# A bias added to the residual rows in the expert groups instead of in the attention windows, and one written order per engine

## The reference

```
x = x + tanh(g_xattn) * gamma * attention(layernorm(x), ctx, ctx)   # 8 heads of 16, softmax over 512
u = layernorm(x)
h = u @ down_w + down_b                                             # 512 -> 256
gate, top 2 of 8 experts = softmax(u @ router_w + router_b - cost)
moe = sum over the two of gate_k * (gelu(gelu(h) @ w1_e + b1_e) @ w2_e + b2_e)  # unchosen experts add a constant
moe = moe + 0.1 * (gelu(gelu(h) @ shared_w1 + b) @ shared_w2 + b)
out = x + tanh(g_ffn) * (moe @ up_w + up_b + gelu(u) @ core_w + core_b)
```

## Time and profile before

| what | value |
|---|---|
| median of 3 runs | 758.85 us (758.62 to 760.65) |
| the profiled execution's own time | 758.85 us |
| its span, first to last instruction | 757.0 us |
| mean granted TensorE clock | 0.992 |
| busy: PE | 699.4 us, 92% |
| busy: DVE | 520.9 us, 69% |
| busy: ACT | 539.5 us, 71% |
| busy: POOL | 487.4 us, 64% |

### The profile page before, as it was taken

One profiled execution on the slowest core, in us unless ns is written; L12 is line 12 of the kernel. 1 busy time (PEld: TensorE's weight loads), 2 busy tenths in 40 slices (PEclk: granted clock), 3 DMA queues, 4 the chain that ended last, 5 costly groups with the idle time before them and its releaser, 6 DMA issues.

```text
span 757.0 us, 20840 instructions
## 1 busy us (share of the span) xinstructions
PE 699.4 (92%) x6134; PEld 379.1 (50%) x6134; DVE 520.9 (69%) x834; ACT 539.5 (71%) x1117; POOL 487.4 (64%) x480
## 2 busy tenths in 40 slices
PE   0699999999999999999898999999999999999978
PEld 0122222333233232223364555588888888888634
DVE  1999998999999999998776456544444444444345
ACT  1389988999999989998765565577667676676311
POOL 5648688888888888868476141346666666566521
PEclk9999999999999999999999999999999999999989
DMA  6545556655565555553437742788889988776666
GB/s 200 201 135 183 187 173 193 206 184 172 196 198 193 190 184 189 177 166 128 127 130 256 263 139 104 248 145 123 123 116 123 124 125 108 101 108 81 144 177 235
DMA packets 137953, 124.04 MB, mean 164 GB/s; under 512 B 70164, under 2 KB 108820, under 8 KB 137880
## 3 DMA queue, kind: packets, MB, share of 16 engines
q1 hardware_dynamic: 123672, 107.50, 49.3%
q0 software_dynamic: 13632, 15.47, 14.2%
q10 hardware_dynamic: 576, 0.13, 0.1%
HBM read 60.39 MB, written 51.53 MB: 148 GB/s over the span
## 4 chain that ended last, share of the span: by engine, by line
PE 61%; DVE 9%; DMA 9%; issue 8%; POOL 6%; ACT 4%; SPq 2%; DVEq 0%; POOLq 0%; ACTq 0%
PE EH L1190 23%; PE Y L1190 15%; PE pv L531 8%; PE ring L518 6%; DVE mx L653 4%; PE nat L506 4%; DMA QS<-q_scratch 3%; ACT P L592 2%; DMA y_sums<-ysb,to 2%; POOL ao L707 1%; SPq L387 1%; DVE statx L635 1%; PE ring L550 1%; DMA q_scratch<-qhl 1%; POOL un L704 1%
## 5 line engine op out<-in xcount | busy, mean ns | idle before, releaser
L653 DVE TENSOR_REDUCE mx<-nat 128x2 f32<-128x1024 f32 x256 | 298.3, 1214 | 31.4 <-PE nat L506 30.4
L592 ACT ACTIVATE P<-ring 128x512 f32<-128x512 f32 x512 | 276.7, 605 | 18.9 <-PE ring L518 11.2
L1956 POOL DMA_INDIRECT y_sums<-ysb,to x84 | 138.2, 1645 | 98.1 <-DVE ysb L1894 85.3
L531 PE MATMUL pv<-P,VT 128*32 128x256 f32 x2048 | 158.5, 393 | 0.3
L506 PE MATMUL nat<-KS,QS 48*128 48x512 f16 x512 | 110.3, 396 | 29.9 <-DMA KS<-k_scratch 16.0
L518 PE MATMUL ring<-QS,KS 49*128 49x512 f16 x512 | 120.9, 391 | 10.3 <-ACT P L592 9.1
L1521 ACT ACTIVATE X<-EH,bcur 128x256 f32<-128x256 f32 x168 | 85.7, 560 | 52.8 <-DVE u L1857 49.0
L1190 PE MATMUL EH<-XA,whi 128*128 128x256 f16 x672 | 116.9, 273 | 0.5 <-DMA XA<-g_rows 0.5
L1190 PE MATMUL Y<-whi,u 128*128 x672 | 116.9, 273 | 0.3 <-DVE u L1857 0.3
L1857 DVE TENSOR_TENSOR u<-X,u 128x512 f16<-128x512 f32 x84 | 57.8, 688 | 78.9 <-ACT u L1527 78.9
L1190 PE MATMUL EH<-XA,wlo 128*128 128x256 f16 x336 | 91.6, 273 | 0.0
(11 more groups left out here) (259 smaller groups left out, 1013.4 us busy)
## 6 DMA issues: line engine op xcount, KB each, us to landing
XA<-in_wall SPq DMA_DIRECT2D x8, 800.0 KB, 4.5
u<-in_wall SPq DMA_DIRECT2D x8, 800.0 KB, 4.4
QS<-q_scratch SPq DMA_DIRECT2D x64, 96.0 KB, 2.3
KS<-k_scratch SPq DMA_DIRECT2D x64, 96.0 KB, 2.4
X<-in_x SPq DMA_DIRECT2D x16, 256.0 KB, 2.7
X<-in_ctx_kv SPq DMA_DIRECT2D x16, 256.0 KB, 3.2
q_scratch<-qhl SPq DMA_DIRECT2D x16, 256.0 KB, 2.1
k_scratch<-khl SPq DMA_DIRECT2D x16, 256.0 KB, 2.2
```

The lines of the kernel that those rows point to most:

```text
L531: m = pe.matmul(pv[32 * j:32 * j + 32, q], VT[i][:, lb, g, j, :], Pb[4 * (s % 2) + j][:, q], start=(lb == 0 and half == 0), stop=(lb == 3) ...
L592: act.activation(Pb[4 * (s % 2) + j][:, :], bank[:, :], ACT.Exp).then_inc(t_use.sem, 1)
L653: dve.tensor_reduce(mx[:, k // 8, :, k % 8], nat[k % 2][:, :, :], AX.X, ALU.max).then_inc(t_max.sem, 1)
L1956: pool.indirect_dma_start(out=ysum[:, :], out_offset=bass.IndirectOffsetOnAxis(ap=to[:, j % 2, a:a + 1], axis=0), in_=ysb[j % 2][:, a, :], ...
```

## The change

- x1t is gone from GpSimd's list. The rows x1 are stored without tb, as soon as x1 is there: the store stands before the load of xr in SP's window, a window's part earlier than the layer norm's u; the last image's is stored before its u instead of after it.
- tb is added on GpSimd by a new operation xb, 128 x 512, one for each of the four images of a stage, on the rows after they were loaded back. In stage 0 the four stand ahead of att of image 14, in stages 1 to 3 behind the eight scatters. VectorE's core waits for xb instead of for the load. The wait for the finished tb moves to the first xb.
- seq has one order for stages 1, 2 and 3. On TensorE y1 of the stage before comes ahead of core2 and core3, and a0, a1, gt behind core3, in the last stage too. On ScalarE acc of the stage before comes ahead of guh, and a and sah behind guh. On VectorE core3 and gul come ahead of sal in the last stage too.

```diff
-            jobs += [(w - 3, n) for n in ("xnegm", "xveps", "xrstd", "u", "x1t")]
+            jobs += [(w - 3, n) for n in ("xnegm", "xveps", "xrstd", "u")]
...
+            if s >= 0:
+                ck.wait(t_pool, s, "x1")
+                sp.dma_start(x1s[ck.index(s)], ao[s % 2][:, :]).then_inc(t_st.sem, 16)
             if t >= 0:
                 ck.wait(t_pool, t - 1, "x1")
                 sp.dma_start(xr[:, :], x[ck.index(t)]).then_inc(t_xr.sem, 16)
...
                 sp.dma_start(us[ck.index(s)], un[:, :]).then_inc(t_us.sem, 16)
-                ck.wait(t_pool, s, "x1t")
-                sp.dma_start(x1s[ck.index(s)], ao[s % 2][:, :]).then_inc(t_st.sem, 16)
...
-            elif what == "x1t":
-                ck.wait(t_pool, b, "u")
-                done(pool.tensor_tensor(ao[i][:, :], ao[i][:, :], keep["tb"][:, :], ALU.add))
...
-                "pool": four("uhp") + [("gh", 0), ("gh", 1)] + four("sc"),
+                "pool": four("uhp") + four("xb") + [("gh", 0), ("gh", 1)] + four("sc"),
...
         if engine == "pe":
-            ahead = cur(four("uT")) + old([("y", 0), ("core", 0)]) + cur([("lg", 0), ("h", 0), ("lt", 0), ("h", 1), ("rk", 0)]) + \
-                (cur([("tot", 0)]) if last else []) + old([("core", 1)]) + cur(four("rt")) + old([("core", 2)])
-            if last:
-                return ahead + shared + old([("y", 1), ("core", 3)]) + cur([("gt", 0), ("y", 0), ("y", 1)])
-            return ahead + old([("core", 3), ("y", 1)]) + shared + cur([("gt", 0)])
+            return cur(four("uT")) + old([("y", 0), ("core", 0)]) + cur([("lg", 0), ("h", 0), ("lt", 0), ("h", 1), ("rk", 0)]) + \
+                (cur([("tot", 0)]) if last else []) + old([("core", 1)]) + cur(four("rt")) + old([("y", 1), ("core", 2), ("core", 3)]) + \
+                cur([("a", 0), ("a", 1), ("gt", 0)]) + (cur([("y", 0), ("y", 1)]) if last else [])
         if engine == "act":
...
-            if last:
-                return ahead + shared + before + cur([("gt", 0)] + four("guh") + [("acc", 0), ("acc", 1)])
-            return ahead + cur(four("guh")) + before + shared + cur([("gt", 0)])
...
+                cur(four("row") + four("gu")) + old([("acc", 0), ("acc", 1)]) + \
+                cur(four("guh") + [("a", 0), ("sah", 0), ("a", 1), ("sah", 1), ("gt", 0)]) + (cur([("acc", 0), ("acc", 1)]) if last else [])
         if engine == "dve":
...
-            if last:
-                return ahead + low + old([("core", 3)]) + cur(four("gul"))
-            return ahead + old([("core", 3)]) + cur(four("gul")) + low
-        return cur([("gh", 0), ("gh", 1)] + four("sc"))
...
+                cur(four("gul") + [("sal", 0), ("sal", 1)])
+        return cur([("gh", 0), ("gh", 1)] + four("sc") + four("xb"))
...
-                wait(dve, t_xx[r % 2], r)
+                wait(dve, t_pool, r, "xb", i)
...
+            elif name == "xb":
+                wait(pool, t_xx[r % 2], r)
+                if r == 0 and i == 0:
+                    pool.wait_ge(t_zp.sem, 2)
+                m = pool.tensor_tensor(xb[r][:, i, :], xb[r][:, i, :], tb[:, :], ALU.add)
...
-                (B - 2, "att"): some(("uhp", 2), ("uhp", 3)), (B - 2, "xnegm"): some("gh")}, rest
+                (B - 2, "att"): some(("uhp", 2), ("uhp", 3), "xb"), (B - 2, "xnegm"): some("gh")}, rest
```

More of the change, by code:

```diff
@@ L474, in last_x1 @@
         def last_x1():
-            sp.wait_ge(t_pool.sem, t_pool.at[B - 1, "x1t"])
+            sp.wait_ge(t_pool.sem, t_pool.at[B - 1, "x1"])
             sp.dma_start(x1s[B - 1], ao[(B - 1) % 2][:, :]).then_inc(t_st.sem, 16)
@@ L756, in last_norm @@
         def last_norm():
-            for what in ("xnegm", "xveps", "xrstd", "u", "x1t"):
+            for what in ("xnegm", "xveps", "xrstd", "u"):
                 job(Clock(pool, 2, t_cst), B - 1, what)
@@ L934, in seq @@
                        [("gl", 0), ("gl", 1)] + R_(route_c) + four("meta") + R_(route_b) + four("gul") + [("sal", 0), ("sal", 1)],
-                "pool": four("uhp") + [("gh", 0), ("gh", 1)] + four("sc"),
+                "pool": four("uhp") + four("xb") + [("gh", 0), ("gh", 1)] + four("sc"),
             }[engine]]
         last = r == NG - 1
-        shared = cur([("a", 0), ("a", 1)])
         if engine == "pe":
-            ahead = cur(four("uT")) + old([("y", 0), ("core", 0)]) + cur([("lg", 0), ("h", 0), ("lt", 0), ("h", 1), ("rk", 0)]) + \
-                (cur([("tot", 0)]) if last else []) + old([("core", 1)]) + cur(four("rt")) + old([("core", 2)])
-            if last:
-                return ahead + shared + old([("y", 1), ("core", 3)]) + cur([("gt", 0), ("y", 0), ("y", 1)])
-            return ahead + old([("core", 3), ("y", 1)]) + shared + cur([("gt", 0)])
@@ L945, in seq @@
-        if engine == "act":
[L946 to L949, removed]
-            if last:
-                return ahead + shared + before + cur([("gt", 0)] + four("guh") + [("acc", 0), ("acc", 1)])
-            return ahead + cur(four("guh")) + before + shared + cur([("gt", 0)])
+            return cur(four("uT")) + old([("y", 0), ("core", 0)]) + cur([("lg", 0), ("h", 0), ("lt", 0), ("h", 1), ("rk", 0)]) + \
+                (cur([("tot", 0)]) if last else []) + old([("core", 1)]) + cur(four("rt")) + old([("y", 1), ("core", 2), ("core", 3)]) + \
+                cur([("a", 0), ("a", 1), ("gt", 0)]) + (cur([("y", 0), ("y", 1)]) if last else [])
@@ L953, in seq @@
+        if engine == "act":
+            return cur([(n, k) for k in range(LB) for n in ("uT", "uh")] + [("lg", 0), ("h", 0), ("h", 1), ("pexp", 1), ("e2", 0)]) + \
+                cur(four("row") + four("gu")) + old([("acc", 0), ("acc", 1)]) + \
+                cur(four("guh") + [("a", 0), ("sah", 0), ("a", 1), ("sah", 1), ("gt", 0)]) + (cur([("acc", 0), ("acc", 1)]) if last else [])
         if engine == "dve":
-            ahead = cur(four("ul")) + old([("core", 0)]) + cur(R_(["lred", "lb", "lmx", "lsub", "lcl"] + route_a) + [("gl", 0)]) + \
+            return cur(four("ul")) + old([("core", 0)]) + cur(R_(["lred", "lb", "lmx", "lsub", "lcl"] + route_a) + [("gl", 0)]) + \
@@ L955, in seq @@
                 cur(R_(route_b) + [("gl", 1)]) + (cur(R_(tables[:2])) if last else []) + cur(R_(route_p + route_c) + four("meta")) + \
-                old([("core", 1)]) + (cur(R_(tables[2:])) if last else []) + old([("core", 2)])
-            low = cur([("sal", 0), ("sal", 1)])
-            if last:
-                return ahead + low + old([("core", 3)]) + cur(four("gul"))
-            return ahead + old([("core", 3)]) + cur(four("gul")) + low
-        return cur([("gh", 0), ("gh", 1)] + four("sc"))
+                old([("core", 1)]) + (cur(R_(tables[2:])) if last else []) + old([("core", 2), ("core", 3)]) + \
@@ L1097, in rest @@
             load_u(2)
+            last_x1()
             last_u()
-            last_x1()
             load_u(3)
@@ L1937, in output_bias @@
             pool.tensor_scalar(tb[:, :], tb[:, :], gate[:, 4:5], 1.0, ALU.mult, ALU.mult).then_inc(t_zp.sem, 1)
-            pool.wait_ge(t_zp.sem, 2)
         def rest():
```

## The result

| what | before | after |
|---|---|---|
| median of the runs shown with the result | 759.38 us (758.62 to 760.65, 4 runs) | 779.00 us (777.16 to 780.84, 4 runs) |
| ratio, after over before | | 1.0257 [1.0230, 1.0285] |
| the profiled execution, own time and span | 758.85, 757.0 us | 778.45, 776.6 us |
| mean granted TensorE clock | 0.992 | 0.978 |

The change makes the kernel 2.6% slower, 19.6 us. The forecast was slower by 9.1 us, 767.9, with a range up to 772: the direction was right, the size was not.

The account below looks back on a forecast made before the run. TensorE, busy almost throughout, was taken as the bound, so only its waits count. 758.85 - 3.3 (attention) - 1.0 (gh) + 6.0 (stages 1, 2) + 5.7 (stage 3) + 1.6 (clock) = 767.9 us, range 756.5 to 772.

Parts of the forecast that it names:

- attention windows and stage 1's gh: Attention: SP's earlier loads end the QS wait, gaining 3.3 us; fewer x1t ahead of stage 1's gh gain 1.0.
- the written order alone: Stages 1 to 3: work placed behind core3 delays TensorE by 0.9, 0.9 and 1.1 us even without collisions.
- xb against gul and sal: Stages 1 to 3: GpSimd's additions hold back VectorE's two-input operations before y0, by 2.1, 2.1 and 4.6 us.
- TensorE's clock: Stage 3: the clock falls behind some 6 us of TensorE idle time before y0, costing 1.6 us.
- I add 1.6 for that: The 1.6 us added for a clock fall at stage 3's idle time before y0.
- the two mid-stage gaps: TensorE idle for 2 us and more before y0 in stages 1 and 2; no clock loss was added.
- Rival (3): Four xb run in one go and the clock also falls at both mid-stage gaps: 773.1 us, chance 0.11.
- Turn by turn: Behind the scatters, gul and xb alternate one operation each, making y0 4.0 us later in each middle stage.
- this hedge: Each middle stage entered the sum at 3.0 us, between 4.0 and 2.8 if a second gul precedes the first xb.
- Rival (4): Attention windows shorten to 20.48 us, 3.7 more gained: 753.8 without collisions, 764.2 with them; chance 0.13.
- Rival (1): Stages 1 to 3: no collisions that count between xb and VectorE, 757.5 us; chance 0.16 together with Rival (2).
- Rival (2): VectorE keeps its run, GpSimd gets in only at its pauses: 758.9 us; chance 0.16 together with Rival (1).

Follow-up runs that it names:

- run 4: The changed kernel without any bias addition and with the earlier orders on TensorE, ScalarE and VectorE: 755.13 us, ratio 0.9961 to the kernel before.
- run 3: The changed kernel with its new orders but without any bias addition: 756.89 us, ratio 0.9984 to the kernel before.
- run 5: The changed kernel with products nobody reads filling TensorE's gaps in stages 2 and 3: 767.88 us, ratio 1.0041 to the kernel before.
- run 11: The changed kernel with 43 unread products between gt and y0 of stage 3 only: 771.45 us, ratio 1.0099 to the kernel before.
- run 2: The changed kernel with the earlier orders on TensorE, ScalarE and VectorE, xb kept behind the scatters: 764.48 us, ratio 1.0088 to the kernel before.
- runs 6 and 7: Each xb waits for the one before it: in the changed kernel 776.58 us, ratio 1.0139; with the earlier engine orders 762.38 us, ratio 0.9975.
- run 12: The changed kernel with the first xb of stages 1 to 3 waiting for VectorE's sal1 of that stage: 764.03 us, ratio 1.0014.
- Run 1: The kernel before with only the changed written orders, bias still added by x1t in the attention windows: 764.91 us, ratio 1.0105.
- run 8: The kernel before with x1 stored behind the next image's loads, and the last x1t and its store behind stage 1's gh: 761.25 us, ratio 0.9962.
- run 9: The kernel before, unchanged, profiled again on another chip: 763.3 us.

## Why the prediction was wrong

| step | forecast | measured |
|---|---|---|
| attention windows and stage 1's gh | -4.3 | -3.0 (run 4; interval -4.3 to -1.6) |
| the written order alone | +0.9, +0.9, +1.1 | +0.7, +0.8, +0.7 (markers of 3 and 4, up to the first expert product); +1.8 in all by the medians |
| xb against gul and sal | +2.1, +2.1, +4.6 in the sum (+3.1, +3.1, +4.6 by its own working) | +3.0, +2.8, +4.2 (markers of 5 and 3, y0 of stage 3) |
| TensorE's clock | +1.6 | +1.6, +2.1, +6.8 (run 5), 11.0 by the mean clock |

**The failed step is the last one: "I add 1.6 for that".** I took the price of the one fall in the profile, a fall behind 1.42 us that lasted some 3 us, as the price of a fall behind 6 us of idle time. It stayed at 1.2 GHz for 17 us, 15 of them from y0 on, through y0, y1 and part of the first expert blocks, and cost 6.8 us (run 5) or 7.0 us (run 11). And I gave the two mid-stage gaps nothing, though I had put them at 2 us and more, longer than the gap of my only example. Rival (3), GpSimd running four xb in one go with the clock falling at these gaps too, is what the profile shows in stages 1 to 3. It had a chance of 0.11 and priced each fall at 1.6 as well, and the range ended at 772, below its 773.1. With 1.6, 2.1 and 6.8 it would have read 773.1 + 0.5 + 5.2 = 778.8; that this is so close to the 779.0 measured is luck, since its other terms (4.3 gained in attention, 4.0 lost in each middle stage) were off in both directions. The rows of before held one fall and no gap of 5 us with the clock behind it, so its length was an unknown cost, and the range should have stayed open there. That the clock was the cause is shown by runs 5 and 11, which only filled the gaps: y0 stayed 8.8 us behind core3 in run 5, and the clock at 1.00.

With these numbers the sum is -3.0, 1.8 to 2.2, 10.0 and 10.5, together 19.3 to 19.7 us, against 19.6 measured. The terms come from different chips, so the closeness is in part luck.

**The collisions were sized nearly right on a picture that did not hold there.** Turn by turn gave 4.0 us for each middle stage, order and collision together, but the sum took 3.0. So it holds 8.8 us of collisions where the working had 10.8 and the runs show 10.0; this hedge is 1.2 us of the miss. Behind the scatters GpSimd did not take turns with VectorE: gul and sal waited for the last of the four xb. The forecast survived because gul and xb all have to be done before sal0 in either picture. Where one short operation meets the row of additions, as in run 2, turn by turn would have said under 2 us and it was 3.97. The Trainium skill (SBUF — State Buffer, section "SBUF: two separate sides") has the shared port as an exclusive lock held for the whole instruction. The trace agrees that one engine blocks the other, but here VectorE got no turn across four instructions (4.93 us); whether GpSimd kept the port or won it again each time no run shows. That a wait between the additions lets VectorE in is shown by runs 6 and 7. But the wait is not always needed: ul and xb took turns without one in run 12 and in stage 0, as I had forecast for gul. Where VectorE was held for all four, they follow the scatters directly; where the engines took turns, they don't. No run tests whether that is the reason.

**The order.** 2.9 us were forecast and 1.8 to 2.2 measured; runs 3 and 4 show it. Run 1's 6.3 us alone would have hidden that.

**Attention.** The mechanism was right and run 8 shows that it is the place in SP's queue. The windows gave 2.5 us of the 3.3 forecast: without QS waits, TensorE waits for ScalarE's P in 24 places (10.7 us, before 17 and 6.2 us), the pair that I had named as late next. Rival (4), windows of 20.48 us, fell: they are 20.85.

**Rival (1)**, the other side, fell: in all three stages xb starts before gul and ends before sal. What decides is what it said, whether xb starts after sal: run 12 does just that and has 1.0014. **Rival (2)**, VectorE keeping its run, fell with the four gul of 5.09 us.

**Open.** Why the end of a TensorE operation is seen up to 4.5 us late on some chips. It needs no xb and no changed order (run 9). The ends of TensorE's operations are modelled in these profiles, so how much of the lateness lies in the records is open too.

## What to carry over

A gap opened in TensorE's work can be paid twice, once as idle time and once at the lower clock behind it. Here the second was the larger for the longest gap: 6.8 us behind 4.93 us of idle time. Before moving an addition of two SBUF operands to GpSimd, look for what VectorE does at that time, and make it start behind VectorE's last operation on the path, or, if only a short operation meets them, try a wait between the additions. A store that waits in a DMA queue ahead of loads can be moved behind them before any arithmetic is moved.

## What the runs showed that I had not expected

- Four GpSimd additions behind the scatters held VectorE's two-input operations off for all of them: one gul 4.78 us, one sal 5.54 us, instead of 0.68. With a wait between them an addition that meets a gul takes 1.5 us instead of 1.27, and a gul 1.72. The same additions took turns with ul without a wait in stage 0 and in run 12.
- TensorE's granted clock stayed at 0.50 for 15 us from y0 on, behind 4.93 us of idle time, and for 16 us behind 3.14 us (run 12). Behind two gaps of about 1 us it fell in one execution (run 1) and held in another; behind 1.36 us it held (run 3).
- 43 useless products of 0.11 us each make the changed kernel 7.0 us faster.
- On two of the three chips of the experiments ScalarE and VectorE saw the end of TensorE's work late, by 0.8 to 4.5 us, in the kernel before too.
